# Attention scores from two stacked products a batch in place of three, with the low part moved to ScalarE and GpSimd

## What is computed

```python
q, k, v = proj(x, Wq), proj(x, Wk), proj(x, Wv)
q = q * min(cond, 4.0)
scores = einsum('bhqd,bhkd->bhqk', q, k) / sqrt(64)
scores = where(causal, scores, most_negative)
attn = softmax(scores)
out = einsum('bhqk,bhkd->bhqd', attn, v)
x = x + einsum('bsd,ed->bse', out, Wo)
```

## Time and profile before

| | |
|---|---|
| median of 3 runs | 1558.01 us (1557.51 to 1558.75) |
| the profiled execution | 1558.96 us |
| its span in the profile | 1557.5 us |
| TensorE busy | 1547.1 us, 99% |
| VectorE, ScalarE, GpSimd busy | 1034.9, 840.9, 866.6 us (66%, 54%, 56%) |

### The profile page before, as it was taken

How to read it: one execution, slowest core, us unless ns; L and a number is a source line. 1 busy time by engine, 2 the same in 40 slices (tenths; PEclk the granted TensorE clock), 3 DMA queues, 4 the chain that set the end, 5 groups by cost and what they waited for, 6 DMA issues and landing times.

```text
span 1557.5 us, 23477 instructions
## 1 busy us (share of the span) xinstructions
PE 1547.1 (99%) x7459; PEld 1302.0 (84%) x7459; DVE 1034.9 (66%) x1891; ACT 840.9 (54%) x2286; POOL 866.6 (56%) x752
## 2 busy tenths in 40 slices
PE   9999999999999999999999999999999989999999
PEld 7888888888888888888888888888888878888887
DVE  5867677664477777777767777777777644555553
ACT  6666566652466666666655666666666622222220
POOL 1555665662365566557655576575577545555552
PEclk9999999999999999999999999999999999999999
DMA  9968988866766677767677466677665696444442
GB/s 324 335 230 278 319 307 296 294 254 231 273 190 198 201 214 209 205 184 191 182 240 229 147 179 202 194 200 200 180 188 157 237 366 226 162 168 163 162 167 83
DMA packets 192300, 341.46 MB, mean 219 GB/s; under 512 B 23986, under 2 KB 116402, under 8 KB 185010
## 3 DMA queue, kind: packets, MB, share of 16 engines
q1 hardware_dynamic: 191026, 331.59, 66.2%
q10 hardware_dynamic: 1152, 8.39, 1.4%
HBM read 184.70 MB, written 134.22 MB: 205 GB/s over the span
## 4 chain that ended last, share of the span: by engine, by line
PE 95%; DVE 2%; DMA 1%; SPq 1%; POOL 0%; issue 0%; ACT 0%; DVEq 0%; POOLq 0%
PE p_PJ L768 22%; PE p_PJ L769 22%; PE p_PJ L770 22%; PE p_SC L770 6%; PE p_SC L769 6%; PE p_SC L768 6%; PE p_PV L873 4%; PE p_LP L768 1%; PE p_PV L768 1%; PE p_PV L770 1%; PE p_PV L769 1%; PE p_LP L770 1%; PE p_LP L769 1%; DVE t_WSL L1285 1%; DVE t_TS L1281 1%; DMA out<-t_xr 0%
## 5 line engine op out<-in xcount | busy, mean ns | idle before, releaser
L769 PE MATMUL p_PJ<-t_XL,t_WH 128*128 128x512 f32 x1008 | 394.2, 391 | 0.0
L768 PE MATMUL p_PJ<-t_XH,t_WH 128*128 128x512 f32 x1008 | 394.2, 391 | 0.0
L770 PE MATMUL p_PJ<-t_XH,t_WL 128*128 128x512 f32 x1008 | 392.1, 389 | 0.0
L1118 ACT ACTIVATE t_PP<-t_PP,t_st 128x128 f32<-128x128 f32 x512 | 199.5, 391 | 174.9 <-DVE t_st L1314 173.3
L1438 POOL TENSOR_TENSOR t_PP<-t_PP,t_st 128x512 f32<-128x512 f32 x128 | 133.2, 1041 | 205.8 <-DVE t_st L1318 205.8
L770 PEld LDWEIGHTS p_PJ<-t_XH,t_WL 128*128 128x128 f32 x1008 | 189.3, 188 | 40.5
L768 PEld LDWEIGHTS p_PJ<-t_XH,t_WH 128*128 128x128 f32 x1008 | 190.0, 188 | 33.8
L769 PEld LDWEIGHTS p_PJ<-t_XL,t_WH 128*128 128x128 f32 x1008 | 190.0, 188 | 32.3
L1332 DVE TENSOR_REDUCE t_AT<-p_PV 64x256 f32<-64x512 f32 x252 | 171.3, 680 | 24.5 <-ACT t_AC L1136 12.1
L1444 POOL TENSOR_TENSOR t_AT<-t_AT,t_AC 128x256 f32<-128x256 f32 x126 | 117.1, 929 | 126.2 <-DVE t_AT L1332 126.2
L1441 POOL TENSOR_TENSOR t_PS<-t_PT,t_PS 128x512 fp32r<-128x512 f32 x122 | 157.6, 1292 | 0.0
(11 more groups left out here) (259 smaller groups left out, 3597.7 us busy)
## 6 DMA issues: line engine op xcount, KB each, us to landing
t_XH<-xth_scratch SPq DMA_DIRECT2D x56, 512.0 KB, 6.4
t_XL<-xtl_scratch SPq DMA_DIRECT2D x56, 512.0 KB, 6.7
t_PT<-t_TB SPq DMA_DIRECT2D x580, 32.0 KB, 2.3
v_scratch<-t_VR SPq DMA_DIRECT2D x64, 256.0 KB, 4.6
xth_scratch<-t_XH SPq DMA_DIRECT2D x16, 1024.0 KB, 4.5
xtl_scratch<-t_XL SPq DMA_DIRECT2D x16, 1024.0 KB, 6.8
t_VX<-v_scratch SPq DMA_DIRECT2D x32, 512.0 KB, 5.6
at_scratch<-t_AT SPq DMA_DIRECT2D x126, 128.0 KB, 3.4
```

The source lines that it names most:

```text
L768: pe.matmul(bank, lh, rh, start=first, stop=False, skip_group_check=goes_on)
L769: pe.matmul(bank, lh, rl, start=False, stop=False, skip_group_check=goes_on)
L770: return pe.matmul(bank, ll, rh, start=False, stop=last, skip_group_check=goes_on)
L1118: act.activation(PP[:, u, h, :], PP[:, u, h, :], ACT.Exp, bias=st[:, 0, u, h:h + 1], scale=1.0, accum_out=st[:, 1, u, h:h + 1]).then_inc(a ...
```

## The change

The scores of a batch come from two matmuls of 256 columns, one for each head, in place of three. For head h, `QM[h]` holds the high part of its 64 rows of Q in those rows and the low part in the other 64. `KM[h]` has K's high part in both halves of the rows (columns 0 to 127) and K's low part in the head's own rows (columns 128 to 255). So the first 128 columns of the result are high x high + low x high and the other 128 are high x low, to be added later.

- ScalarE: K's high part in three activations of 64 rows in place of two; Q's high part in two of 64 rows in place of one of 128; and for each batch a new one that scales the second 128 columns of both heads into `PP` (`low_at`).
- GpSimd: for each batch a new addition of the mask to `PP` (`add_at`).
- VectorE: Q's low part in two instructions of 64 rows in place of one; one more copy of K's high part out of the bank; the scaling instruction now adds `PP` in place of the mask, and each is followed by its row maximum at once (before, two and two).
- The scores lie in three banks by turns (`SC[0]`, `SC[1]`, `LP`), a whole bank a batch, and from the fourth on TensorE waits for the masked result of the batch three before. It waits for all three activations and all three VectorE instructions of K.
- The tables: `a` is 7 units behind the end of K (5 before); the instructions of the four batches are spread out; the Q high part stands at +6 and its low part at +7, K's high part at +9.25 and its low part at +10.

```diff
-                late = 2.5 if n else 0
+                late = 5 if n else 0
                 q_ev.put(done + late, n)
                 ql_ev.put(done + late + 1, n)
                 done += 8
                 kh_ev.put(done + 0.25, n)
                 kl_ev.put(done + 1, n)
-                a = done + 5
+                a = done + 7
                 for u in range(GB):
-                    k = u // 2
-                    sc_at.put(a + k, GB * n + u)
-                    mask_at.put(a + 1 + 2 * k, GB * n + u)
-                    exp_at.put(a + (2, 3, 4, 5)[u], GB * n + u)
-                move_at.put(a + 10, n)
+                    sc_at.put(a + (0, 0.5, 1, 4.5)[u], GB * n + u)
+                    low_at.put(a + (0.75, 1.25, 1.75, 5.25)[u], GB * n + u)
+                    add_at.put(a + (1.25, 2, 3, 6)[u], GB * n + u)
+                    mask_at.put(a + (2.5, 3.5, 4.5, 7.25)[u], GB * n + u)
+                    exp_at.put(a + (3.5, 4.5, 5.5, 8.25)[u], GB * n + u)
+                move_at.put(a + 12.5, n)
...
-                    recip_at.put(a + 4 + 2 * k, P)
-                    norm_at.put(a + 4.25 + 2 * k, P)
-                    turn_at.put(a + 7.5 + 1.5 * k, P)
+                    recip_at.put(a + (6.25, 9.25)[k], P)
+                    norm_at.put(a + (6.5, 9.5)[k], P)
+                    turn_at.put(a + (9, 12)[k], P)
                     last = n == 4 * NGRP - 1
-                    half_at.put(a + (20 if last else 25.25) + 0.5 * k, P)
-                    ptl_at.put(a + (20.75 if last else 26) + 1.5 * k, P)
-                    v = a + (27.25 + 3.25 * k if last else 29 + 4.5 * k)
+                    half_at.put(a + (22.5 if last else 26) + 0.5 * k, P)
+                    ptl_at.put(a + (23.25 if last else 26.5) + 1.5 * k, P)
+                    v = a + (29.25 + 3.25 * k if last else 29 + 4.5 * k)
...
+            if U >= 3:
+                pe.wait_ge(dve_s, U - 2)
+            for h in range(2):
+                mm = pe.matmul(s_bank(U)[:, h].rearrange("p l k -> p (l k)"), QM[h][:, cols], KM[h][:, u, :], start=True, stop=True)
+            mm.then_inc(pe_sc, 1)
...
+                    act.activation(PP[:, u], s_bank(U)[:, :, 1], ACT.Copy, scale=beta[:, bb:bb + 1]).then_inc(act_l, 1)
...
                     for h in range(2):
-                        r, k = slice(64 * h, 64 * h + 64), slice(128 * h, 128 * h + 128)
-                        dve.wait_ge(act_k, 2 * n + h + 1)
-                        dve.tensor_tensor(KL[r, :, k], pj[r], KH[r, :, k].bitcast(f32), ALU.subtract).then_inc(dve_k, 1)
+                        r = slice(64 * h, 64 * h + 64)
+                        dve.wait_ge(act_k, 3 * n + h + 2)
+                        dve.tensor_tensor(KM[h][r, :, 128:256], pj[r], KM[h][r, :, 0:128].bitcast(f32), ALU.subtract).then_inc(dve_k, 1)
+                    dve.tensor_copy(KM[1][0:64, :, 0:128], pj[64:128]).then_inc(dve_k, 1)
...
+                    dve.wait_ge(pool_m, U + 1)
+                    dve.scalar_tensor_tensor(out=PP[:, u], in0=s_bank(U)[:, :, 0], scalar=beta[:, bb:bb + 1],
+                                             in1=PP[:, u], op0=ALU.mult, op1=ALU.add).then_inc(dve_s, 1)
...
+                    pool.wait_ge(act_l, U + 1)
+                    pool.tensor_tensor(PP[:, U % GB], PP[:, U % GB], mask[:].unsqueeze(1).to_broadcast([128, 2, 128]), ALU.add).then_inc(pool_m, 1)
```

More of the change, by code:

```diff
@@ L162, in cond_attention @@
             LATE = tile
[L163 to L166, removed]
+        KM = [sb(f"KM{h}", [128, GB, 256], f32r) for h in range(2)]
+        QM = [sb(f"QM{h}", [128, T], f32r) for h in range(2)]
         with nc.sbuf_tensor("t_PS", [128, 8, 2, 128], f32r) as tile:
@@ L237, in cond_attention @@
         step_at, sc_at, pv_at = At(), At(), At()
-        mask_at, exp_at, recip_at, norm_at, turn_at, move_at, half_at, ptl_at, other_at, own_at, at_at = (At() for _ in range(11))
+        low_at, add_at, mask_at, exp_at, recip_at, norm_at, turn_at, move_at, half_at, ptl_at, other_at, own_at, at_at = (At() for _ in range(13))
         q_ev, ql_ev, kh_ev, kl_ev, v_ev, v_store, v_split = (At() for _ in range(7))
@@ L460, in cond_attention @@
             t = T_PAIR + PAIR * q
-            early = t - PAIR
+            early = t - PAIR + (5 if q == 0 else 0)
             yp_load.put(T_END + (24, 24.25)[q] if q < 2 else t - PAIR - 8, q)
@@ L857, in pe_scores @@
                 pe.wait_ge(dve_g, 5 * (NP - 2))
-            z = u // 2
-            three(SC[z][:, 256 * (u % 2):256 * (u % 2) + 256], QH[:, cols], QL[:, cols], KH[:, u, :], KL[:, u, :], True, True).then_inc(pe_sc, 1)
+            if U == 2:
+                pe.wait_ge(dve_X, 2 * B)
+            if U >= 3:
[3 more added lines that the diff above has]
+            mm.then_inc(pe_sc, 1)
         def pe_values(U):
@@ L1104, in act_program @@
                         r = slice(64 * h, 64 * h + 64)
-                        act.activation(KH[r, :, 128 * h:128 * h + 128], pj[r], ACT.Copy).then_inc(act_k, 1)
+                        other = slice(64 - 64 * h, 128 - 64 * h)
+                        act.activation(KM[h][r, :, 0:128], pj[r], ACT.Copy).then_inc(act_k, 1)
+                        if h == 0:
+                            act.activation(KM[h][other, :, 0:128], pj[r], ACT.Copy).then_inc(act_k, 1)
                 for n in q_ev(tick):
@@ L1112, in act_program @@
                             act.wait_ge(s_x1[z], 16 * x1_stores(z))
-                    act.activation(QH[:], PJ[bank_of["q", n]][:], ACT.Copy).then_inc(act_q, 1)
+                    for h in range(2):
+                        r = slice(64 * h, 64 * h + 64)
+                        act.activation(QM[h][r], PJ[bank_of["q", n]][r, :], ACT.Copy).then_inc(act_q, 1)
+                for U in low_at(tick):
+                    n, u = divmod(U, GB)
+                    bb = GROUP[n // NC] * GB + u
+                    act.wait_ge(pe_sc, U + 1)
+                    if U == 0:
+                        act.wait_ge(dve_beta, 1)
+                    if n and u == 0:
+                        act.wait_ge(dve_t, 2 * n)
+                    act.activation(PP[:, u], s_bank(U)[:, :, 1], ACT.Copy, scale=beta[:, bb:bb + 1]).then_inc(act_l, 1)
                 for U in exp_at(tick):
@@ L1292, in dve_program @@
                     for h in range(2):
-                        r, k = slice(64 * h, 64 * h + 64), slice(128 * h, 128 * h + 128)
-                        dve.wait_ge(act_k, 2 * n + h + 1)
-                        dve.tensor_tensor(KL[r, :, k], pj[r], KH[r, :, k].bitcast(f32), ALU.subtract).then_inc(dve_k, 1)
+                        r = slice(64 * h, 64 * h + 64)
+                        dve.wait_ge(act_k, 3 * n + h + 2)
+                        dve.tensor_tensor(KM[h][r, :, 128:256], pj[r], KM[h][r, :, 0:128].bitcast(f32), ALU.subtract).then_inc(dve_k, 1)
+                    dve.tensor_copy(KM[1][0:64, :, 0:128], pj[64:128]).then_inc(dve_k, 1)
                 for n in ql_ev(tick):
-                    dve.wait_ge(act_q, n + 1)
-                    dve.tensor_tensor(QL[:], PJ[bank_of["q", n]][:], QH[:].bitcast(f32), ALU.subtract).then_inc(dve_q, 1)
+                    for h in range(2):
+                        r, other = slice(64 * h, 64 * h + 64), slice(64 - 64 * h, 128 - 64 * h)
+                        dve.wait_ge(act_q, 2 * n + h + 1)
+                        dve.tensor_tensor(QM[h][other], PJ[bank_of["q", n]][r, :], QM[h][r].bitcast(f32), ALU.subtract).then_inc(dve_q, 1)
                 for U in mask_at(tick):
@@ L1432, in pool_program @@
                     pool.tensor_tensor(v_low(VV[j % 2], u), by_heads(VX[:, u, :]), v_high(VV[j % 2], u).bitcast(f32), ALU.subtract).then_inc(pool_vl, 1)
+                for U in add_at(tick):
+                    if U == 0:
+                        pool.wait_ge(l_const, 32)
+                    pool.wait_ge(act_l, U + 1)
+                    pool.tensor_tensor(PP[:, U % GB], PP[:, U % GB], mask[:].unsqueeze(1).to_broadcast([128, 2, 128]), ALU.add).then_inc(pool_m, 1)
                 for P in norm_at(tick):
@@ L1730, in sp_program @@
                 if tick == 0:
-                    sp.dma_start(mask[:], mask_d).then_inc(l_mask, 16)
-                    sp.dma_start(beta[:], cond.to_broadcast([128, B])).then_inc(l_cond, 16)
+                    sp.dma_start(mask[:], mask_d).then_inc(l_const, 16)
+                    sp.dma_start(beta[:], cond.to_broadcast([128, B])).then_inc(l_const, 16)
                 for bb in l0_load(tick):
```

29 lines of the change are left out of this document (12 added, 17 removed).

## The result

The changed kernel takes 1954.0 us (median of 4 runs, 1952.9 to 1955.2), the kernel before 1558.4 us (4 runs, 1557.5 to 1559.4) on the same chip. The ratio is 1.254, 95% interval 1.252 to 1.256. The forecast was 1887, the range 1790 to 1960. The profiled execution took 1953.45 us, with a span of 1952.1.

What follows compares the result with a forecast made beforehand. TensorE bounded the kernel before; the change was to bind it by a queue loop. Attention 1133 us against 838 (+295) and drain +3 made 1857 us; clock +30 made 1887, range 1790 to 1960.

Steps and rivals of the forecast that it cites:

- the clock: TensorE at 1.2 GHz after its 4.1 us waits: 89 us if in every cell; a third of cells taken, 30 us.
- the branch to which the prediction gave 0.18: Loop as followed, clock down in nearly all cells, or with contention: 1915 to 1960, about 1946 us; chance 0.18.
- the one with 0.58: Loop as followed, clock falling in few or some cells: 1790 to 1915, forecast 1887 us; chance 0.58.
- The saving: TensorE: four 256-column matmuls fewer a cell, 0.47 us, 30 us over 64 cells.
- The loop: Attention cell, mask 0 to next mask 0 through all engines' queues: 16.85 us plain, 18.52 with V splits.
- The whole stage: Attention stage, 63 cells at full clock: 1133 us against 838, so +295 us.
- that rival, at 1946 us: Clock low in nearly all cells, or contention: 1915 to 1960, about 1946 us; chance 0.18.
- V splits: GpSimd, 32 cells: two splits ahead of the even sum add 1.67 us; a fallen clock adds only 0.6 there.
- the sum of 1.3 us: GpSimd, 16 cells: a 1.31 us sum between additions 0 and 1 makes exp 1 come 1.15 us later.
- The ends: Drain behind the last cell: longer softmax and two units more cover, +3 us; opening and output stages as before.
- Addition and VectorE: GpSimd's 256-column addition kept at 0.75 us; at 1.24, 1.0 us more a cell, 62 in all.

Runs made afterwards that it cites:

- new_tables_no_low: Changed kernel with the tables of new_tables_b and K's low part left out of the scores (no scaling activations, no mask additions on GpSimd): 1563.1 us, ratio 1.0044.
- warm: Changed kernel plus 16 unused 512-column matmuls on TensorE ahead of its wait for the even products: 1866.3 us, ratio 1.198.
- old_work_new_order: Kernel before with all its own instructions, including three score matmuls, but the change's tables: 1789.7 us, ratio 1.148.
- own_rows_first: Changed kernel with the odd own rows put ahead of K's low part and copy in VectorE's queue: 1866.8 us, ratio 1.198.
- own_rows_and_high_first: Changed kernel with odd own rows ahead of K low and, on ScalarE, P's high part ahead of exp 3 and K high: 1763.1 us, ratio 1.131.
- new_tables_b: Changed kernel's instructions with other tables only: odd own rows ahead of K low, Q and K evictions later, score 3 at +2.5: 1589.6 us, ratio 1.021.
- extra_on_loop: Changed kernel plus two VectorE additions of 128 x 176 a cell between K's copy and the odd own rows: 2006.8 us, ratio 1.288.

## Why the prediction was right, and what was mis-sized

The mechanism was right link by link. The point forecast was 67 us low, nearly all of it in one term, the clock; the result lies 6 us inside the upper end of the range, in the branch to which the prediction gave 0.18 and not in the one with 0.58.

- **The saving** of 0.47 us a cell was right, and shows where nothing waits: 12.85 us in `new_tables_no_low`. In the changed kernel it is hidden in an idle engine.
- **The loop** stands in the cell above. At full clock it takes 17.15 us against 16.85 forecast, 18.45 against 18.52 with V splits. Most of the 0.3 us are starts a little further apart than I had them: exp 3 to K high took 0.90 us (749.59 to 750.49) against 0.78 and a hand-over, the copy 0.72 to the next start, and the products came 0.15 us behind the own rows. The low part took 0.47 us (forecast 0.40), the addition 0.74 (0.75), the copy 0.69 (0.68).
- **The whole stage** without the clock: 1133 us forecast, (1538.3 - 397.6) = 1140.7 in `warm`.
- **The clock** is the term that was mis-sized, "I take a third of the cells, 30 us". It fell behind all but the first (428.95, a wait of 3.54 us) of TensorE's 62 waits of over 3 us in the stage, and cost 1226.0 - 1140.7 = 85 us, against 89 forecast for that case: that rival, at 1946 us, had a chance of 0.18 and is what happened. One row with a wait of 3.95 us and a fallen clock, and 4.1 us forecast, spoke for all cells rather than for a third; I had no row for the third. (By the earlier trace rows itself the level was back after 5.7 us rather than about 5: 0.91 over the window from 1268 leaves 0.7 us at 0.50.) `warm` shows that it is the clock and not something beside it.
- **V splits** cost nothing in the changed kernel, as the 0.6 us in that term has it: forecast 18.52 + 0.6 and 16.85 + 2.26 are the same 19.1. TensorE's slow steps and GpSimd's splits lie beside one another. Twelve of the 16 cells with the sum of 1.3 us are 20.55 us (831.74 to 852.28 and 852.28 to 872.83 between K's copies), 1.2 over the 19.35 that the three in a row have on average; in `warm`, at full clock, such cells are 1.1 longer (forecast 1.15).
- **The ends** of the kernel took 726.1 us (1952.1 - 1226.0) against 719.8 before, +6 for a forecast of +3.
- **Addition and VectorE**: GpSimd's addition stayed at 0.74 us, so the bound of 1.24 wasn't needed.
- What was **missed** is the second chain right beside the loop: the parts of P behind K high. It doesn't show in the time of the change, but I expected 1740 to 1830 us when one link was cut and got 1867. The expectation for both links cut was met at 1763 with a wait and a clock that it had wrong.

The sum: 30 us forecast for the clock were 85 (+55), the loop +8, the ends +3; together 66 of the 67 us between 1887 and 1954.

## What to carry to other kernels

When work is taken off the bounding engine and put on others, first follow the queues once round, from one instruction to the same one of the next tile: the sum of what is strung there, not the busy time of an engine, is the new floor. Look for an instruction that frees something for the old bound (here own rows, 1.4 us of work) and see what the new order puts ahead of it. A periodic wait of TensorE like those here has to be priced with its slower clock in nearly every period (61 of 62 at about 4 us, 49 of 61 at 2.2 us), and after one link is cut the next chain, often close behind, sets the time.

## What the runs showed of the hardware

- **The clock's changes keep no distance to the work.** In the three cells above it came back 3.3, 5.2 and 6.2 us behind the start of the even products, and the cells from K copy to K copy are 18.64, 19.46 and 19.94 us, over and over, though the kernel's own work repeats by four. A microsecond at 1.2 GHz costs 1 - 0.227/0.427 = 0.47 us, by the paces of 512-column matmuls at both levels. An estimate from this and the 17.15 us of `warm`: 18.7, 19.6 and 20.0. In `warm`, where the clock stays up, the pattern of three is gone. So it is the clock's. The Trainium skill (TensorE: Matmul & The Clock Gate, Part 1) says that the gate's windows are free-running; the trace agrees as far as the return goes. That some equal waits would end at the higher level, as I read it in the prediction, no wait of 4.0 us showed, but the 2.2 us waits of `old_work_new_order` did: 49 ended at the lower level and 12 at the higher one.
- **The clock fell behind shorter waits, too**: all of 2.9 us in `own_rows_first`, 49 of 61 of 2.2 us in `old_work_new_order`, and some of 1.8 us in `own_rows_and_high_first`. Waits of 0.4 to 0.7 us in `warm` and `new_tables_b` left it at full level.
- **A wait that ends just in time still costs.** The weight load of the first scores brings in Q, which is long there, but it stands behind the same wait for K as its matmul. In `new_tables_b` the load and the matmul of the first scores start together, where loads otherwise start 0.1 to 0.2 us ahead of their matmul:

```profile
905.08 0.39 PE L770 MATMUL p_PJ<-t_XH,t_WL 128*128 128x512 f32 x1
905.44 0.50 PE L867 MATMUL p_SC<-t_KM,t_QM 128*128 128x256 f32 x2
905.78 0.40 PE L768 MATMUL p_PJ<-t_XH,t_WH 128*128 128x512 f32 x1
...
905.44 0.30 PEld L867 LDWEIGHTS p_SC<-t_KM,t_QM 128*128 128x128 f32 x2 [0.40 <-DVE t_KM L1319]
```

  From 905.08 to 905.78 are 0.70 us for one 512-column and two 256-column matmuls, which take 0.23 + 2 x 0.12 = 0.47 by the earlier trace rows. That is 0.23 us with no idle time shown for PE. In all but two of the 62 cells this stretch took 0.61 to 0.71 us, and without such a wait it mostly took 0.46 (`new_tables_no_low`). By an estimate, 62 x 0.23 = 14 us of the 31 by which this kernel is slower than before.
- **VectorE beside GpSimd.** A VectorE addition of 128 x 176 elements with both inputs in SBUF took 0.33 us alone, 0.61 where GpSimd's low part of P ran during 0.41 of it, and up to 1.43 where GpSimd ran during 1.22 of it (`extra_on_loop`). In the changed kernel, whose scaling instruction has one input in SBUF, GpSimd's additions stayed between 0.72 and 0.75.
